# Layer normalisation of a hybrid block in token-tile groups, centred by a matrix product, with three score banks

## The reference, cut to what matters

```python
x = x + _L0_conv_ref(_gn(x), ...)      # softmax over 7x7 taps, weights from two small 1x1 layers
t = _to_tokens(x)                      # [4, 3136, 64]
t = t + _L1_attn_ref(_ln_t(t), ...)
t = t + _L1_ffn_ref(_ln_t(t), ...)     # top 2 of 8 experts

def _ln_t(v, eps=1e-05):
    m = jnp.mean(v, axis=-1, keepdims=True)
    s = jnp.var(v, axis=-1, keepdims=True)
    return (v - m) / jnp.sqrt(s + eps)

# in _L1_attn_ref, x the normalised tokens
scores = a[:, :, None] + b[:, None, :] + c      # a = x.wa, b = x.wb, c = (x*wc).x
attn = jnp.einsum('bij,bjf->bif', jax.nn.softmax(scores, axis=2), x)
# then gates z, r, f from [x, attn]; result r*x + f*z
```

## Time and profile before

| | us |
|---|---|
| median of 3 timed runs | 2125.78 (2124.56 to 2127.0) |
| profiled execution | 2119.56 |
| its span, first to last instruction | 2117.7 |
| TensorE products busy in it | 1804.3 (85%) |
| VectorE busy | 1324.4 (63%) |
| ScalarE busy | 1165.0 (55%) |
| GpSimd busy | 576.3 (27%) |

### The profile page before, as it was taken

The page is one execution under the profiler, slowest core; times in us unless marked ns, Lnnn a source line. Parts: engine busy times, 40 slices in busy tenths (PEclk is TensorE's granted clock), DMA queues, the critical chain, the costliest instruction groups (busy, mean ns, idle before and its releaser), DMA issues. The chain is left out here.

```text
span 2117.7 us, 31951 instructions
## 1 busy us (share of the span) xinstructions
PE 1804.3 (85%) x11571; PEld 623.2 (29%) x11571; DVE 1324.4 (63%) x1785; ACT 1165.0 (55%) x1535; POOL 576.3 (27%) x294
## 2 busy tenths in 40 slices
PE   4467877777653799999999999999887698999998
PEld 1011111111102233333333333333333242333333
DVE  2259999999977766666666666666345536343343
ACT  3799999999423344434444434443433555566665
POOL 0898888888303000000000000000012131222222
PEclk9799999999876799999999999999988899999999
DMA  2220121112111110000000000100020101000000
GB/s 89 90 104 34 62 77 46 41 68 78 66 63 72 36 31 9 10 10 10 5 9 10 10 9 5 40 9 9 10 75 1 31 1 44 7 9 7 9 9 9
DMA packets 22821, 69.57 MB, mean 33 GB/s; under 512 B 4912, under 2 KB 12336, under 8 KB 21296
## 3 DMA queue, kind: packets, MB, share of 16 engines
q1 hardware_dynamic: 22560, 67.00, 9.7%
q10 hardware_dynamic: 144, 0.96, 0.1%
HBM read 47.78 MB, written 13.62 MB: 29 GB/s over the span
## 5 line engine op out<-in xcount | busy, mean ns | idle before, releaser
L1143 DVE TENSOR_REDUCE at_mpart<-at_ps_m 112x1 f32<-112x448 f32 x784 | 453.8, 624 | 181.6 <-PE at_ps_m L867 180.0
L988 ACT ACTIVATE at_prob<-at_ps_s 128x896 f32<-128x896 f32 x336 | 304.7, 917 | 459.6 <-PE at_ps_s L878 459.6
L419 DVE TENSOR_TENSOR cm_prod<-cm_ps_ev,win 128x1792 f32<-128x1792 f32 x196 | 388.3, 2018 | 13.1 <-ACT cm_ps_ev L470 9.5
L368 POOL TENSOR_TENSOR cm_diff<-front 128x1792 f32<-128x1792 f32 x98 | 320.6, 3277 | 69.3 <-POOLq L113 39.1
L1569 ACT ACTIVATE ge_hid<-ge_ps,ffn 128x448 f32<-128x448 f32 x448 | 251.0, 635 | 157.8 <-PE ge_ps L1436 157.0
L867 PE MATMUL at_ps_m<-front,vh 128*112 128x448 f16 x784 | 297.7, 381 | 23.5 <-DVE at_mpart L1143 6.7
L894 PE MATMUL at_ps_a<-at_prob,win 128*64 128x448 f32 x1344 | 295.9, 554 | 0.0
L576 PE MATMUL cm_ps_acc<-cm_prod,cst 128*32 128x504 f32 x1568 | 218.6, 630 | 76.2 <-DVE cm_prod L419 45.9
L878 PE MATMUL at_ps_s<-vh,front 128*128 (+3 forms) x700 | 247.7, 354 | 0.2 <-DMA vh<-at_mrow 0.2
L878 PE MATMUL at_ps_s<-vl,front 128*128 (+3 forms) x700 | 247.4, 353 | 0.0
L1753 POOL MEMSET wt<- 128x6272 f16 x1 | 5.3, 5325 | 853.3 <-POOLq L771 853.3
(11 more groups left out here) (189 smaller groups left out, 1737.7 us busy)
## 6 DMA issues: line engine op xcount, KB each, us to landing
win<-x_dram SPq DMA_DIRECT2D x28, 868.0 KB
at_rden<-rden_dram SPq DMA_DIRECT2D x28, 224.0 KB, 3.2
x_dram<-win SPq DMA_DIRECT2D x4, 962.0 KB
conv_out<-cm_cout SPq DMA_DIRECT2D x28, 112.0 KB, 3.9
win<-x SPq DMA_DIRECT2D x2, 1568.0 KB, 13.0
t_dram<-front SPq DMA_DIRECT2D x2, 1568.0 KB, 5.4
front<-attn SPq DMA_DIRECT2D x8, 392.0 KB, 6.0
front<-t_dram SPq DMA_DIRECT2D x2, 1568.0 KB, 8.6
```

Source lines behind the costliest of these rows:

```text
L368: pool.tensor_tensor(diff[:, s % ND, 0:n, :].rearrange("p n (r c) -> p n r c", c=W), a.rearrange("p n (r c) -> p n r c", c=W), b, ALU.subt ...
L419: v.tensor_tensor(prod[:, hs, :, 0:CH].rearrange("p s (r c) -> p s r c", c=W), ev.rearrange("p s (r c) -> p s r c", c=W), wv, ALU.mult).th ...
L988: act.activation(prob_of(s)[0:w, 0:a, :], ps_s[0:w, (s + 1 - par) % 2, 0:a, 0:CH], ACT.Exp).then_inc(exp_done, 1)
L1143: v.tensor_reduce(mpart[:, e // NCH, e % NCH:e % NCH + 1], ps_m[0:NORM, (e + par) % 2, 0:CH], AX.X, ALU.max).then_inc(rough_max, 1)
```

## The change

It has five parts.

- GpSimd adds the 2688 early columns of both pairs at the end of its stream in `conv_main`; VectorE keeps the 448 late ones. TensorE's first five groups wait for the early addition alone.
- The turn is a true product with a constant matrix `centre`, which is I - 1/64 for each image's 64 channels: what comes out is turned and centred. `means` and `centre` are gone. ScalarE copies a group and takes its squares from the same bank.
- Pair 0 runs group by group: turn, copy and square, variance, power, multiplication, turn back, copy and `hi`, `lo`, the engines' streams shifted against each other by one to three groups.
- Pair 1 is normalised within step (0, 0): in slot s its group s is turned and group s - 3 turned back. ScalarE's `hi` of pair 1 comes after this step.
- The rough scores rotate through three banks of `ps_m` and so wait for the maximum three places back. Their third bank is taken from `ps_a`, which has one bank left: the sums of a step wait for `block_out` of the step before. The transposed maxima use bank 1, the projection bank 2. Each image waits for its own two transfers of `stack`.

```diff
+                early = slice(0, PIX - CH)
+                for t in range(PAIRS):
+                    pool.wait_ge(tres_in[t], 32)
+                    pool.tensor_tensor(tres[:, t, early], tres[:, t, early], xa[:, t, early],
+                                       ALU.add).then_inc(early_added, 1)
...
-        ps_m = psum("at_ps_m", [128, 2, BANK])
-        ps_a = psum("at_ps_a", [128, 2, BANK])
+        ps_m = psum("at_ps_m", [128, RB, BANK])
+        ps_a = psum("at_ps_a", [128, BANK])
...
+                    if g == 0:
+                        pe.wait_ge(early_added, t + 1)
+                    if g == (PIX - CH) // (GROUP * TT):
+                        pe.wait_ge(added, t + 1)
...
-                        ins = pe.transpose(ps_m[0:w, (t * NG + g) % 2, (n % GROUP) * 128:(n % GROUP) * 128 + 128],
-                                           tres[:, t, n * TT:n * TT + w], mat("ident"))
+                        ins = pe.matmul(turn_bank(t, g)[0:w, (n % GROUP) * 128:(n % GROUP) * 128 + 128],
+                                        tres[:, t, n * TT:n * TT + w], mat("centre"), start=True, stop=True)
...
-                    if e >= 2:
-                        pe.wait_ge(rough_max, i * RO + e - 1)
-                    elif e == 0 and not (b == 0 and isinstance(q, int) and q == 0):
+                    begin = b == 0 and isinstance(q, int) and q == 0
+                    if e >= RB:
+                        pe.wait_ge(rough_max, i * RO + e - RB + 1)
+                    elif e == TURN_BANK and not begin:
                         pe.wait_ge(top_half, i)
-                    elif e == 1 and before(b, q, 1)[0] in range(B - 1):
+                    elif e == PROJECT_BANK and not begin and before(b, q, 1)[0] in range(B - 1):
                         pe.wait_ge(vl_done, i + NCH)
...
-                        elif s == 0 and not (isinstance(n, int) and n == 1):
-                            pe.wait_ge(sums_out, n - 1)
+                        elif s == 0:
+                            pe.wait_ge(sums_out, n)
...
-                pe.wait_ge(spread[0], 64)
...
+                    if b < B and isinstance(q, int) and q == 0:
+                        pe.wait_ge(spread[b], 32)
...
+                        if not attend:
+                            if s == 0:
+                                pe.wait_ge(vl_done, NCH)
+                            if s < NG:
+                                turn(1, s)
+                            if 0 <= s - BACK_AFTER < NG:
+                                turn_back(1, s - BACK_AFTER)
...
+                    act.activation(sq[0:w, here, :].rearrange("p n c -> p (n c)"),
+                                   turn_bank(t, g)[0:w, 0:128 * len(tiles)], ACT.Square).then_inc(turned_out, 1)
...
-                means(0)
-                centre(0)
-                means(1)
-                variance(0)
-                centre(1)
-                variance(1)
-                normalize(0)
-                normalize(1)
-                second_half(0)
+                for g in range(NG + 3):
+                    if g < NG:
+                        variance(0, g)
+                    if 1 <= g <= NG:
+                        normalize(0, g - 1)
+                    if g >= 3:
+                        lower(g - 3)
...
+                        if step == (0, 0) and e % PER_SLOT == PER_SLOT - 1:
+                            if e // PER_SLOT < NG:
+                                variance(1, e // PER_SLOT)
+                            if 1 <= e // PER_SLOT <= NG:
+                                normalize(1, e // PER_SLOT - 1)
...
+    put("centre", np.kron(np.eye(2, dtype=f), np.eye(C, dtype=f) - f(1.0 / C)))
```

More of the change, by code:

```diff
@@ L712, in attention @@
         split = sem("at_split")
-        spread = [sem(f"at_spread{t}") for t in range(PAIRS)]
+        spread = [sem(f"at_spread{b}") for b in range(B)]
         v_done = sem("at_v_done")
@@ L765, in before, with turn_bank, back_bank, group_rows @@
             return (b - 1, NCH + q - n) if isinstance(q, int) and q < n else (b, q - n)
+        def turn_bank(t, g):
+            return ps_m[:, g % 2, :] if t == 0 else ps_s[:, 0, g % 2, :]
+        def back_bank(t, g):
+            if t == 0:
+                return ps_a if g % 2 else ps_m[:, RB - 1, :]
+            return ps_s[:, 1, g % 2, :]
+        def group_rows(g):
+            return tile_tokens(group_tiles(g)[-1])
+        def group_columns(g):
+            tiles = group_tiles(g)
+            return slice(tiles[0] * TT, tiles[0] * TT + sum(tile_tokens(n) for n in tiles))
         def first_bank(k):
@@ L937, in body @@
                                 for a in range(len(tiles(back))):
-                                    sums(late, i - 2, par, back, a)
+                                    sums(late, i - 2, back, a)
                         if rough:
@@ L993, in turn_out @@
+                    if step == (0, 0):
+                        first_half(1)
                 def turn_out(t, g):
                     tiles = group_tiles(g)
-                    w = tile_tokens(tiles[-1])
+                    w = group_rows(g)
+                    here = slice(tiles[0], tiles[-1] + 1)
                     act.wait_ge(turned, t * NG + g + 1)
-                    act.copy(xT[0:w, t, tiles[0]:tiles[-1] + 1, :].rearrange("p n c -> p (n c)"),
-                             ps_m[0:w, (t * NG + g) % 2, 0:128 * len(tiles)]).then_inc(turned_out, 1)
@@ L1000, in square @@
-                def square(t):
-                    act.wait_ge(centred, t + 1)
-                    act.activation(sq[t], xT[:, t, :, :], ACT.Square).then_inc(squared, 1)
+                    act.copy(xT[0:w, t, here, :].rearrange("p n c -> p (n c)"),
+                             turn_bank(t, g)[0:w, 0:128 * len(tiles)])
+                    if t > 0:
+                        act.wait_ge(var_done, g + 1)
+                    act.activation(sq[0:w, here, :].rearrange("p n c -> p (n c)"),
+                                   turn_bank(t, g)[0:w, 0:128 * len(tiles)], ACT.Square).then_inc(turned_out, 1)
@@ L1004, in turn_back_out @@
                 def turn_back_out(t, g):
-                    tiles = group_tiles(g)
-                    n = sum(tile_tokens(a) for a in tiles)
+                    at = group_columns(g)
+                    bank = back_bank(t, g)[:, 0:at.stop - at.start]
                     act.wait_ge(back, t * NG + g + 1)
-                    act.copy(xhat[:, t, tiles[0] * TT:tiles[0] * TT + n],
-                             ps_a[:, (t * NG + g) % 2, 0:n]).then_inc(back_out, 1)
+                    act.copy(xhat[:, t, at], bank).then_inc(back_out, 1)
@@ L1011, in first_half @@
+                    if t == 0:
+                        act.activation(hi[t][:, at], bank, ACT.Identity, bias=vec("one"),
+                                       scale=vec("keep")).then_inc(hi_done, 1)
                 def first_half(t):
@@ L1028, in _ @@
                     query_half(0, k, k, first_bank(k))
-                for g in range(NG):
-                    turn_back_out(1, g)
                 steps(act, body)
@@ new lines, in normalize, with lower @@
+                def normalize(t, g):
+                    at = by_row(xT[:, t, :, :], g)
+                    v.wait_ge(rstd_done, t * NG + g + 1)
+                    v.tensor_tensor(at, at, rstd[0:group_rows(g), t, rows(g)].unsqueeze(2).broadcast_to(list(at.shape)),
+                                    ALU.mult).then_inc(normed, 1)
+                def lower(g):
+                    at = group_columns(g)
+                    v.wait_ge(hi_done, g + 1)
+                    v.scalar_tensor_tensor(out=lo[0][:, at], in0=back_bank(0, g)[:, 0:at.stop - at.start],
+                                           scalar=vec("keep"), in1=hi[0][:, at], op0=ALU.mult,
+                                           op1=ALU.subtract).then_inc(split, 1)
@@ L1150, in body @@
                             invert(i - 2)
+                    if step == (0, 0):
+                        ones(1).then_inc(ready, 1)
                     if b < B:
@@ L1163, in _ @@
                 last = (B - 1, NCH - 1, B * NCH - 1)
-                block_out(*last, 1 - B % 2)
+                block_out(*last)
                 invert(last[2])
```

153 lines of the change are left out of this document (73 added, 80 removed).

## The result

| | before | changed |
|---|---|---|
| median of the timed runs | 2125.17 us (2120.33 to 2127.0) | 2062.15 us (2061.36 to 2063.16) |
| profiled execution | 2119.56 us, span 2117.7 | 2061.42 us, span 2059.6 |
| first cast of maxima / last / rest of the span | 721.6 / 1502.8 / 614.9 us | 695.2 / 1440.8 / 618.8 us |

The ratio is 0.9711, with the interval 0.9698 to 0.9723: 3% faster. The forecast had been 2070 us.

The account below looks back on a forecast made before the run. Attention was taken as bound by TensorE's in-order stream, behind a serial normalisation. Gains of 24 and 32 us, 56 in sum, took the profiled 2119.56 to 2063.6; plus 6.2 gave 2069.8, forecast 2070 us, range 2052 to 2096.

Parts of the forecast that it names:

- The head: From the normalisation ahead of attention through step (0, 0): first score at 699.5 instead of 723.69, 24 us net, bounds 12 and 31.
- The first rough score: Start of step (0, 0): at 668 instead of 702 us, bounds 665 and 676, after projections and two transfers.
- Two transfers: Ahead of step (0, 0): only image 0's transfers are waited for, two instead of four, put at 7 us.
- The projections: After pair 0's pipeline, from 660: 7 x 0.75 us and two evacuations, until 667.
- Step (0, 0) itself: First attention step, with pair 1 normalised inside: VectorE's work 27.7 us against 18.55 before; 34 at half clock.
- the rival of half clock: TensorE's clock stays low before and in step (0, 0): gain there only 9 to 12 us, 2084 us; chance 0.10.
- the banks: Steady attention steps: third rough-score bank gains, single accumulator bank costs; net 32 us, bounds -5 and 43.
- the 1.4 us that this rule would have added to the forecast: Pair 0's pipeline: seven small GpSimd powers waiting behind VectorE multiplications, at most 0.2 us a group; forecast would be 2071.
- The early additions: End of the convolution: GpSimd adds 2688 columns of both pairs, 5.3 us each, 10.6 together, hidden in its idle time.
- The steady step: Attention steps after the first: 1.3 us shorter in 20 steps, 0.9 in the last image's 7, 32 us in all.
- The new wait: Each step's first sums wait for VectorE's copy of the previous step's sums: 0.55 to 0.6 us, 0.15 to 0.2 lost.
- From the profile to the median: Conversion to timed runs: profiled 2063.6 us plus the 6.2 us between profile and median before gives 2069.8.

Follow-up runs that it names:

- The head alone: Changed kernel with the banks of before (two for rough scores, two for sums), everything else of the change kept: 2108.55 us, ratio 0.9937.
- the low half first: Changed kernel with VectorE's low half of group g - 3 put first in each round of pair 0's pipeline: 2063.38 us, ratio 0.9713.
- the turn first on the early copy: Changed kernel with sums copied after the third maximum and, in step (0, 0), pair 1's turn ahead of the slot's rough scores: 2053.34 us, ratio 0.9662.

## Why the prediction was right, and where it was off

**The head** was forecast at 24 us and gave 26.4. The first rough score was put at 668 (bounds 665 and 676) and came at 669.27; the last maximum at 696, and it ended at 694.6; the first score at 699.5, and it ran at 697.27. But the first number came about by another path than the one forecast. Step by step: the pipeline ended at 661.5, where 660.5 had been said. Two transfers, put at 7 us, were to release the first rough score at 668; it was the last projection that did. The projections had been priced by the earlier trace rows at full clock and were to be through, with their evacuations, at 667; half of them ran at half clock, the 14 took 7.81 us, and with the last evacuation it was 669. That the two paths end so near each other is luck. Step (0, 0) itself was put at 27.7 us and took 25.3: the slot is 2.99 us rather than 3.3, because I had added 0.35 us of small operations and starts to each, where the rows show 0.17 and starts that overlap. Had TensorE stayed at 1.2 GHz there, the rival of half clock might have come up; the granted clock was 1.00 from 669 to 695 us.

**Whose gain it is** the prediction had wrong. It booked all of the 24 us to the new head and all of the 32 to the banks. The head alone gives 13.9 us in span. The step that failed is the cost of TensorE in a slot of step (0, 0), the sum of its busy times (2.4 us against VectorE's 3.3). Busy time leaves out that the turn stands in order behind a rough score that waits for a bank. With two banks a slot took 5.23 us instead of 3.3, part of it at half clock. The forecast held because the change brings both parts.

**Power.** Eight columns were put at 1.67 us. Timeline of GpSimd, the first three powers of the pipeline and two in step (0, 0):

```profile
642.19 4.89 POOL L855 TENSOR_TENSOR at_rstd<-at_var,at_mhalf 128x8 f32<-128x8 f32 x3 [5.21 <-DVE at_var L1105]
...
673.27 1.63 POOL L855 TENSOR_TENSOR at_rstd<-at_var,at_mhalf 128x8 f32<-128x8 f32 x1 [16.05 <-DVE at_var L1105]
675.66 2.01 POOL L855 TENSOR_TENSOR at_rstd<-at_var,at_mhalf 128x8 f32<-128x8 f32 x1 [0.75 <-DVE at_var L1105]
```

The one at 673.27, beside maxima that read PSUM, took 1.63 us. The next began 0.17 us after VectorE's multiplication of 0.69 us at 675.49, and took 2.01. The Trainium skill (SBUF — State Buffer, section Who interferes with whom) has such a pair of operations exclude each other; the trace agrees in kind, with 0.38 us. It does not agree where the power begins just ahead of the multiplication. The second and third of the three in the pipeline do, beside multiplications at 643.87 and 645.48; the three took 4.89 / 3 = 1.63 us each and the multiplications 0.69 and 0.71. In step (0, 0) nobody waited for a power; in the pipeline VectorE did twice, for 0.16 and 0.49 us. So of the 1.4 us that this rule would have added to the forecast, at most 0.65 us show as waiting.

**The early additions** took 5.93 and 5.90 us instead of 5.3, and were covered as forecast. Priced by the earlier trace rows, a line's mean over another shape, they came out 11% too low.

**The steady step** was forecast to shrink by 1.3 us in 20 steps and by 0.9 in 7, 32 us in all; it was 35.6. The distances of the casts show 29.2 - 27.9 = 1.3 us with projections and 28.18 - 27.12 = 1.06 in the last image. Step (0, 1) is 2.9 us shorter, and I had priced it like the others. 1.6 of this belongs to the head and not to the banks: with the head alone that step takes 26.71 us instead of 28.32, at a granted clock of 1.00 instead of 0.89. The clock has a part in it, for with the additions back on VectorE, and nothing else changed in this step, it takes 26.17 us at 0.94 instead of 25.42 at 1.00. The new wait was put at 0.55 to 0.6 us and a pair of slots at 5.0; they are 0.53 and 4.96.

**From the profile to the median.** 56 us gave 2063.6 for the profiled execution, which took 2061.42. To this I added the 6.2 us by which before's median lies above its profile, and this is the largest error: the changed kernel's median is only 0.7 us above its own. 5.5 of the 7.9 us of miss are here.

**After the last cast** 3.9 us were lost in code that the change doesn't touch. This rest of the span, before and after:

```profile
1503.00:2117.70 614.70, 557.88 (x2670) 211.26 (x2666) 269.59 (x390) 327.65 (x559) 127.02 (x89) 0.95 0.07 18
```

```profile
1441.00:2059.60 618.60, 563.12 (x2670) 212.12 (x2666) 268.82 (x390) 327.94 (x559) 126.83 (x89) 0.94 0.07 18
```

The same 2670 products took TensorE 5.2 us longer, the other engines the same. Over the kernels measured this rest is 615 to 621 us, with no relation to what was edited; why the clock falls differently there stays open.

## What to carry to other kernels

A PSUM bank is best placed where the in-order engine meets its producer most often: here a third bank for 28 scores a step was worth about 1.8 us a step (1.3 net and the 0.5 that follows), and the second accumulator, given up for it, cost 0.5, of which 0.4 came back by moving the copy that frees it. Read the cost of too few banks from distances between issues and from the number of products in a stretch; among the waits look at those of the weight loads, since the products' own hide it. Before two parts of a change are priced apart, ask in which order the shared engine issues them: work on which another engine depends belongs ahead of the instruction that waits.

## What was not expected of the hardware

- With less work on TensorE (transposes for products), its granted clock in the head was lower (0.54 from 643 to 674 us), and the head no shorter (34.3 against 33.65 us). This is one profile.
- A busy share of 97.5% (633.90 of 650 us) still held 4.7% of room, since waits for a bank lie partly inside the modelled durations.
- In the kernel with the head alone the clock fell again in the midst of step (0, 0), after TensorE had stood idle 2.25 and then 2.85 us in two slots. In the changed kernel, where no wait at a rough score there exceeds 0.77 us, it stayed up. Such long waits are not needed for it: with the low half first (granted clock 0.93 from 671 to 697 us) and with the turn first on the early copy (0.82 from 670.4 to 696.7) it fell as well, with waits of at most 0.8 and 0.7 us at the rough scores. What brings it down stays open. With three banks it cost little in this step, 26.3 us at 0.82 and 25.9 at 0.93, against 25.9 at 1.00, since VectorE is the bound.
